# Masking the causal scores with pairs of half-array products of 256 columns

## The chip, the cores and the metric

The kernel runs on one core of one Trainium2 chip. The metric is the device time of one execution in microseconds (us). The engines are TensorE (PE, matmuls; PEld are its weight loads), VectorE (DVE), ScalarE (ACT), GpSimd (POOL) and SyncE (SP, which issues most DMAs). They run side by side and wait for each other on semaphores. TensorE's clock has two levels, 1.2 and 2.4 GHz; the profile gives the granted clock as a share of full speed.

## The reference

There are 32 sequences of 128 tokens with 128 features. Two layers follow each other, each a cross-attention to a context (16 heads of 8 features) and an expert network, and each adds to x. Only the second attention is causal:

```python
Q = (query @ Wq + bq).reshape(B, Tq, H, Hd).transpose(0, 2, 1, 3)
K = (key @ Wk + bk).reshape(B, Tk, H, Hd).transpose(0, 2, 1, 3)
scores = jnp.einsum('bhqd,bhkd->bhqk', Q, K) / scale
causal = jnp.triu(jnp.ones((Tq, Tk), bool), k=1)
scores = jnp.where(causal[None, None], -jnp.inf, scores)
attn = jax.nn.softmax(scores, axis=-1)
out = jnp.einsum('bhqk,bhkd->bhqd', attn, V)
...
x = x + _L0_xattn_ref(_layernorm(x), ctx_1024, ctx_1024, ...)
x = x + _L0_ffn_ref(_layernorm(x), ...)       # each token to one of 8 experts
x = x + _L1_xattn_ref(_layernorm(x), ctx_1024, ctx_1024, ...)   # causal
x = x + _L1_ffn_ref(_layernorm(x), ...)       # each token to two of 8 experts
```

## The kernel before, in words

The program has six parts, each a block that all engines enter and leave together: `prepare` (loads weights, makes constants), `project` (queries, keys and values), `attention(0)`, `experts0`, `attention(1)`, which is the causal one, and `experts1`. The order of the instructions is written out by hand in each engine's function. Semaphores alone hold the engines together.

`prepare` fills `ident4` (four identity matrices of 128x128 side by side, bf16) and `future` (row k, column q holds -1e30 where key k lies behind query q, else 0). SP issues 18 loads there and waits for them. PE then turns the weights over, DVE copies them out, and the block ends when the last engine is done.

In `attention(l)` the loop runs over n, the sequence. At step n, PE makes the scores of sequence n + 3 and the probabilities' products of sequences n and n - 1. A sequence is done in two units u = 0 and 1 of eight heads each. The steps of a unit are:

- `scores(n, u)` on PE. It waits for `max_s`, the maxima of the unit before, since all units share the two PSUM banks `s_pair`. In the causal layer a mask product comes first: for each of the two banks (four heads each), `future` as stationary operand by `ident4`, 128 rows and 512 columns (L628). Then come eight score products of 128 columns (L633), in pairs: `half(0, ...)` uses rows 0 to 63 of the array and writes bank 0, `half(1, ...)` uses rows 64 to 127 and writes bank 1. They add to the mask.
- `reduce_pair(n, u)` on DVE (L861) takes each row's maximum from the 1024 columns. It signals `max_s`.
- `scores_t(n, u)` on PE makes the same scores with keys on the rows (L654) and adds minus the maxima (L657), again in half-array pairs. It waits until the exponentials have freed its two banks.
- `exponential` on ACT (L763), `mask` on POOL (L1029, which sets the future to zero once more), and `mix` on PE (L670), the product with the values.

Between them stand the turning of the maxima (L642), of the outputs (L681, L688) and the output projection (L692). From the sixth sequence on, the routing of the second expert network is worked in, in batches of four sequences: L700, L706 on PE, a row of short DVE steps (L898 to L947), and scattered writes from POOL (L1058).

The names in the profile drop digits, so that `ident` in a row of L628 is `ident4`, and `rrrk` is `ranked`.

Of the kernel before, what the change touches and what calls it, by code (L numbers as in the profile page):

```python
# [136 lines left out]
def build(nc, a, out):  # L137
# [3 lines left out]
    def sem(name):  # L141
        in_use.append(nc.alloc_semaphore(name=name))
        return in_use[-1]
# [10 lines left out]
    with ctx:  # L154
        def sb(name, shape, dt=F32, to=ctx):
            return to.enter_context(nc.sbuf_tensor(name, shape, dt))
# [12 lines left out]
        ident = sb("ident", [128, 128])  # L169
        ident4 = sb("ident4", [128, 4, 128], BF16)  # L170
        future = sb("future", [128, 128], BF16)
        earlier_tokens = sb("earlier_tokens", [128, 128], BF16)
        all_tokens = sb("all_tokens", [128, 128], BF16)
        tile_no_i, tile_no = sb("tile_no_i", [128, SLOTS], I32), sb("tile_no", [128, SLOTS])
# [47 lines left out]
        def prepare():  # L222

            loaded, zeroed = sem("p_loaded"), sem("p_zeroed")
            turned, kept, made, counted = sem("p_turned"), sem("p_kept"), sem("p_made"), sem("p_counted")
            picked = sem("p_picked")
            with ExitStack() as own, nc.Block() as block:
                w_raw = [sb(f"w_raw{i}", [128, D], to=own) for i in range(4)]
                qk_raw = [sb(f"qk_raw{i}", [128, D], to=own) for i in range(2)]
# [14 lines left out]
                @block.sync  # L244
                def _(sp):
                    for to, src in loads:
                        sp.dma_start(to, src, allow_slow_non_contiguous=True).then_inc(loaded, 16)
                    sp.wait_ge(loaded, 16 * len(loads))

                @block.gpsimd  # L250
                def _(pool):
# [288 lines left out]
        def attention(l):  # L540
# [13 lines left out]
            with ExitStack() as own, nc.Block() as block:  # L554
# [41 lines left out]
                def half(a, rows):  # L596
                    return slice(a * HALF, a * HALF + rows)
# [5 lines left out]
                @block.sync  # L603
                def _(sp):
                    def load(g):
                        sp.wait_ge(st_ps, (g - QK_BUFS + 1) * G * PAIRS)
                        for side in "kq":
                            load_side(sp, l, g, side, qk_in[g % QK_BUFS])

                    for g in range(QK_BUFS, NG):  # L610
                        load(g)
                    for g in range(NG - QK_BUFS, NG):
                        sp.wait_ge(qk_in[g % QK_BUFS], g // QK_BUFS * QK_IN)

                @block.tensor
                def _(pe):
                    def scores(n, u):

                        buf, t = columns(n)
                        if u == 0 and n % G == 0:  # L620
                            if n // G < QK_BUFS:
                                pe.wait_ge(early_in[l], QK_BUFS * QK_IN)
                            else:
                                pe.wait_ge(qk_in[buf], n // G // QK_BUFS * QK_IN)
                        pe.wait_ge(max_s, earlier(n * PAIRS + u))
                        if causal:
                            for a in range(2):
                                pe.matmul(s_pair[:, a * 512:(a + 1) * 512], future[:],  # L628
                                          ident4[:].rearrange("p a b -> p (a b)"), start=True, stop=False,
                                          skip_group_check=True)  # L630
                        for j in range(C4):
                            for a in range(2):
                                mm = pe.matmul(s_pair[:, (a * C4 + j) * T:(a * C4 + j + 1) * T],  # L633
                                               qq[buf][half(a, PROD), u * C4 + j, t], kk[buf][half(a, PROD), u * C4 + j, t],
                                               start=not causal, stop=True, skip_group_check=causal)
                        mm.then_inc(s_ps, 1)
# [1027 lines left out]
```

## Time and profile before

| | |
|---|---|
| times of three runs | 892.91, 894.95, 895.14 us; median 894.95 |
| profiled execution | 895.08 us, of which the span is 893.3 |
| PE / PEld busy | 670.4 / 458.0 us |
| DVE / ACT / POOL busy | 483.9 / 385.5 / 347.6 us |
| L628, as many as are recorded | 98 matmuls of 128x512, 35.1 us, mean 417 ns |
| causal attention | 428 to 627 us of the span |

The profile is one execution. Busy time of PE is modelled from where a matmul starts and how long its columns take, so that starts are a better measure than durations: two matmuls that overlap both show their full latency. Some matmul records are missing. In the rows below, the bracket at the end names how long the engine was idle before the instruction and what ended that idle time; "issue" is idle time without a waited-for event. A row with "x2" or "x8" merges instructions, and its first number is the start of the first.

### The profile page before, as it was taken

What the parts mean: (1) busy time and instruction counts of PE and PEld (TensorE: products, weight loads), DVE (VectorE), ACT (ScalarE), POOL (GpSimd) and SP (SyncE); (2) the same over time, 40 slices, a digit from 0 to 9 for tenths busy, and PEclk for the clock granted to TensorE, in tenths of its full rate; (3) what the DMA queues carried; (4) which work ended last, traced back from release to release, by engine and by line L of the source; (5) the groups of instructions that cost most, each with busy time, mean ns of one, the idle gap of its engine ahead of it and who ended that gap; (6) DMA issues with size and microseconds to landing.
All of it is one profiled execution on the core that took longest, in us unless ns stands there. A gap on an engine that the chain in (4) does not pass through costs nothing. (4 is left out here: it accounts for less than half of the span.)

```text
span 893.3 us, 21719 instructions
## 1 busy us (share of the span) xinstructions
PE 670.4 (75%) x7687; PEld 458.0 (51%) x7717; DVE 483.9 (54%) x1275; ACT 385.5 (43%) x948; POOL 347.6 (39%) x506
## 2 busy tenths in 40 slices
PE   1566648898996898994499999998406999999910
PEld 1343326676774454541155666665304877787700
DVE  1687446676772677773356888887341222222213
ACT  0344325575774012121056666667303665666500
POOL 4354240010011134342034477778841544455410
PEclk9988677899998899997589999999556999999965
DMA  3459831464302999999014333300111222212027
GB/s 95 132 152 182 209 114 24 80 108 81 74 3 38 208 239 209 216 219 228 7 23 77 72 90 87 84 26 26 43 36 48 59 55 61 58 55 64 28 72 222
DMA packets 93273, 87.17 MB, mean 98 GB/s; under 512 B 7785, under 2 KB 87921, under 8 KB 90097
## 3 DMA queue, kind: packets, MB, share of 16 engines
q1 hardware_dynamic: 84592, 74.70, 38.9%
q0 software_dynamic: 4352, 8.99, 3.2%
q10 hardware_dynamic: 4224, 2.10, 0.8%
q8 instruction: 65, 1.06, 0.5%
q14 instruction: 40, 0.32, 0.1%
HBM read 43.99 MB, written 41.76 MB: 96 GB/s over the span
## 5 line engine op out<-in xcount | busy, mean ns | idle before, releaser
L861 DVE TENSOR_REDUCE nm<-bank 128x8 f32<-128x1024 f32 x128 | 156.5, 1223 | 63.8 <-PE bank L633 61.7
L763 ACT ACTIVATE pr<-bank 128x512 f32<-128x512 f32 x256 | 147.2, 604 | 85.0 <-PE bank L657 82.2
L1572 DVE TENSOR_TENSOR exac<-bank,exsi 128x352 f32<-128x352 f32 x72 | 37.8, 525 | 127.8 <-PE bank L1479 121.0
L1029 POOL TENSOR_SCALAR_AFFINE_SELECT pr<-pr 128x1024 f32<-128x1024 f32 x64 | 69.7, 1088 | 75.3 <-ACT pr L763 75.1
L1451 POOL DMA_INDIRECT results<-exy,exre x72 | 70.8, 983 | 33.0 <-issue 33.0
L670 PE MATMUL bank<-pr,values 128*9 128x128 f32 x2048 | 82.3, 280 | 1.7 <-POOL pr L1029 1.7
L654 PE MATMUL bank<-qq,kk 48*128 48x128 bf16 x1024 | 76.8, 223 | 6.4 <-issue 4.2
L1308 PE MATMUL bank<-e0ch,expert_w 128*128 128x512 f32 x128 | 71.9, 644 | 8.2 <-DVE e0ch L1220 8.1
L657 PE MATMUL bank<-mt,pick 64*128 64x128 bf16 x1024 | 76.8, 223 | 0.0
L633 PE MATMUL bank<-kk,qq 48*128 48x128 bf16 x1024 | 55.5, 233 | 19.5 <-DVE nm L861 8.0
L1058 POOL DMA_INDIRECT sorted_in<-rrrow,rrpli x64 | 63.2, 988 | 14.2 <-issue 14.0
L1493 PEld LDWEIGHTS bank<-down_w,exat 128*128 128x128 f32 (+1 forms) x432 | 58.9, 191 | 18.3 <-issue 6.7
L633 PEld LDWEIGHTS bank<-kk,qq 48*128 48x128 bf16 x1024 | 31.4, 100 | 66.9 <-issue 38.6
L1493 PE MATMUL bank<-down_w,exat 128*128 (+1 forms) x432 | 60.4, 276 | 1.9 <-ACT exat L1535 1.9
L1476 PE MATMUL bank<-gate_w,exxt 128*128 x144 | 57.9, 485 | 0.9 <-ACT exxt L1524 0.8
L628 PE MATMUL bank<-ident,future 128*128 128x512 bf16 x98 | 35.1, 417 | 28.2 <-DVE bank L985 11.1
L654 PEld LDWEIGHTS bank<-qq,kk 48*128 48x128 bf16 x1024 | 52.1, 98 | 7.9 <-issue 4.5
L1479 PE MATMUL bank<-up_w,exxt 128*128 x144 | 55.6, 469 | 0.0
L1036 POOL CAST mp<-nm 128x16 bf16<-128x16 f32 x32 | 6.3, 196 | 126.3 <-DVE nm L861 122.0
L657 PEld LDWEIGHTS bank<-mt,pick 64*128 64x128 bf16 x1024 | 52.3, 98 | 2.3 <-issue 2.3
L1544 ACT ACTIVATE exy<-bank,exsh 128x128 f32<-128x128 f32 x72 | 26.4, 367 | 61.5 <-PE bank L1493 52.4
L670 PEld LDWEIGHTS bank<-pr,values 128*9 128x9 f32 x2048 | 43.9, 91 | 15.6 <-POOL pr L1029 2.2
(203 smaller groups left out, 1304.3 us busy)
## 6 DMA issues: line engine op xcount, KB each, us to landing
sorted_in<-padding SPq DMA_DIRECT2D x8, 2145.0 KB
k_parts<-pj_parts SPq DMA_DIRECT2D x16, 384.0 KB, 2.9
kk<-k_parts SPq DMA_DIRECT2D x32, 192.0 KB
qq<-q_parts SPq DMA_DIRECT2D x32, 192.0 KB
exx<-sorted_in SPq DMA_DIRECT2D x72, 65.0 KB
kk<-k_parts SPq DMA_DIRECT2D x32, 128.0 KB
qq<-q_parts SPq DMA_DIRECT2D x32, 128.0 KB
coy<-results SPq DMA_DIRECT2D x8, 512.0 KB, 4.7
```

The source lines that it names most:

```text
L633: mm = pe.matmul(s_pair[:, (a * C4 + j) * T:(a * C4 + j + 1) * T], qq[buf][half(a, PROD), u * C4 + j, t], kk[buf][half(a, PROD), u * C4 + ...
L654: pe.matmul(to[a][:, j * T:(j + 1) * T], kk[buf][half(a, PROD), u * C4 + j, t], qq[buf][half(a, PROD), u * C4 + j, t], start=True, stop=Fa ...
L657: mm = pe.matmul(to[a][:, j * T:(j + 1) * T], pick[half(a, HALF), u * C4 + j, :], max_t[n % 3][half(a, HALF), :], start=False, stop=True, ...
L670: mm = pe.matmul(o_bank[32 * j:32 * j + VW, c * T:(c + 1) * T], values[l][:, n, c % 2 * H2 + c // 2 * C4 + j, :], probs[c][:, j * T:(j + 1 ...
L763: act.activation(probs[c], st_bank[(n * NC + c) % ST][:], ACT.Exp, scale=scale).then_inc(exp_s, 1)
L861: dve.tensor_reduce(neg_max[n % 2][:, u * 2 * C4:(u + 1) * 2 * C4], s_pair.rearrange("q (h k) -> q h k", k=T), AX_X, ALU.max, negate=True) ...
L1029: pool.affine_select(out=probs_pair[u][:], in_=probs_pair[u][:], compare_op=ALU.is_ge, fill=0.0, base=0, pattern=[[0, 2 * C4], [1, T]], ch ...
L1058: pool.indirect_dma_start(sorted_in[:], bass.IndirectOffsetOnAxis(ap=place_i[bt.p][:, k, b:b + 1], axis=0), row[bt.p][:, k, b, :], None).t ...
L1308: pe.matmul(y_bank[:], expert0_w[:, e, :], chosen[e % 2][:], start=(e == 0), stop=(e == E - 1)).then_inc(y_ps, 1)
L1451: pool.indirect_dma_start(results[:], bass.IndirectOffsetOnAxis(ap=result[q.g.p][:, q.b:q.b + 1], axis=0), y_g[q.p][:], None).then_inc(y_o ...
L1476: pe.matmul(gate_bank[q.p][:, 0:F], x, gate_w[:, bass.ds(e, 1), :].rearrange("d e f -> d (e f)"), start=True, stop=True).then_inc(gate_ps, 1)
L1493: mm = pe.matmul(y_bank[q.p][:, 0:D], acts_t[q.p][0:fn, f * T:(f + 1) * T], down_w[0:fn, bass.ds(e, 1), f, :].rearrange("f e d -> f (e d)" ...
```

## The change

The mask product of a unit is written as four matmuls of 64 rows and 256 columns. Each bank's mask is cut by keys: turn 0 covers keys 0 to 63 of each of the four heads, turn 1 covers keys 64 to 127. In each turn the half a = 0 of the array (rows 0 to 63) writes bank 0 and the half a = 1 (rows 64 to 127) writes bank 1. The stationary operand is `future_h`, which holds both 64-row halves of `future` on both halves of the partitions; the moving operand is `ident4h`, four identities of 64x64 on both halves. Both are filled in `prepare` by six small DMAs of SP, for which SP waits before it leaves the block.

```diff
@@ build
+        ident4h = sb("ident4h", [128, 4, HALF], BF16)
+        future_h = sb("future_h", [128, 2, 128], BF16)
@@ prepare, block.sync
                     sp.wait_ge(loaded, 16 * len(loads))
+                    sp.wait_ge(made, 4)
+                    for a in range(2):
+                        to = slice(a * HALF, (a + 1) * HALF)
+                        for k in range(2):
+                            of = slice(k * HALF, (k + 1) * HALF)
+                            sp.dma_start(future_h[to, k, :], future[of, :]).then_inc(halved, 16)
+                        sp.dma_start(ident4h[to, :, :], ident4[0:HALF, :, 0:HALF]).then_inc(halved, 16)
+                    sp.wait_ge(halved, 96)
@@ attention, block.tensor
+                    def hide(pair, of):
+                        for turn in range(2):
+                            for a in range(2):
+                                to = pair[a].rearrange("p (j c) -> p j c", c=T)
+                                pe.matmul(to[:, :, half(turn, HALF)], of[half(a, HALF), turn, :], ident4h[half(a, HALF), :, :],
+                                          start=turn == 0, stop=False, skip_group_check=True)
@@ scores
                         if causal:
-                            for a in range(2):
-                                pe.matmul(s_pair[:, a * 512:(a + 1) * 512], future[:],
-                                          ident4[:].rearrange("p a b -> p (a b)"), start=True, stop=False,
-                                          skip_group_check=True)
+                            hide([s_pair[:, a * 512:(a + 1) * 512] for a in range(2)], future_h)
```

On PE, one unit of the causal attention before, with the end of the unit ahead of it. L670 are the products with the values, L628 the mask, L633 the scores, L654 and L657 the transposed scores:

```order
L642 MATMUL bank<-ident,mp 128x128
L670 MATMUL bank<-pr,values 9x128 x8
L628 MATMUL bank<-ident,future 128x512 x2
L633 MATMUL bank<-kk,qq 128x128 x8
L654 MATMUL bank<-qq,kk 128x128 x2
L657 MATMUL bank<-mt,pick 128x128 x2
```

The same place after. The lines have moved by the inserted ones: L657, L685, L632, L648, L669 and L672 answer to the six above.

```order
L657 MATMUL bank<-ident,mp 128x128
L685 MATMUL bank<-pr,values 9x128 x8
L632 MATMUL bank<-ident4h,future_h 128x4x64 x4
L648 MATMUL bank<-kk,qq 128x128 x8
L669 MATMUL bank<-qq,kk 128x128 x2
L672 MATMUL bank<-mt,pick 128x128 x2
```

The mask stands where it stood, and four narrower products take the place of two.

On SP, the end of `prepare` before, with the last load, and the first load of `project`:

```order
L247 DMA bo1<-L1_xattn_bo 128x128
L227 UNCONDITIONAL_BRANCH [waits p_loaded]
L378 UNCONDITIONAL_BRANCH [waits barrier_Pool_Activation_PE_DVE_SP_release]
L382 DMA pj_c0<-ctx_1024 128x4x128 [waits pj_c_turned]
```

And after:

```order
L249 DMA bo1<-L1_xattn_bo 128x128
L256 DMA future_h<-future 64x128 [waits p_made,p_loaded]
L256 DMA future_h<-future 64x128
L257 DMA ident4h<-ident4 64x4x64
L256 DMA future_h<-future 64x128 x2
L257 DMA ident4h<-ident4 64x4x64
L229 UNCONDITIONAL_BRANCH [waits p_halved]
L388 UNCONDITIONAL_BRANCH [waits barrier_Pool_Activation_PE_DVE_SP_release]
L392 DMA pj_c0<-ctx_1024 128x4x128 [waits pj_c_turned]
```

Six DMAs and one wait have come between the last load and the end of the block.

## Rows read from the trace of the kernel before

Times in the timelines are the start and the duration in us from the span's start. The rows by stretch give the stretch and its length, then busy us (and instructions) of PE, PEld, DVE, ACT and POOL, the granted clock, the share of the DMA engines and GB/s.

**Rows 1.** Busy time by stretch of the causal attention.
```profile
428.00:453.00 25.00, 15.65 (x145) 6.70 (x149) 10.43 (x15) 3.11 (x9) 1.91 (x2) 0.52 0.00 1
...
457.00:497.00 40.00, 37.87 (x695) 24.34 (x703) 26.86 (x63) 25.06 (x66) 17.50 (x18) 1.00 0.41 77
...
497.00:609.00 112.00, 101.44 (x1833) 68.17 (x1846) 99.08 (x281) 70.49 (x183) 80.82 (x86) 1.00 0.29 65
...
609.00:627.00 18.00, 13.98 (x257) 10.12 (x255) 11.67 (x48) 12.92 (x31) 14.91 (x16) 1.00 0.09 29
```

**Rows 2.** Timeline of the opening: start us, us, engine, line, op, tiles.
```profile
431.16 1.04 PE L628 MATMUL bank<-ident,future 128*128 128x512 bf16 x2 [1.39 <-DVE nm L861]
...
432.13 0.61 PE L633 MATMUL bank<-kk,qq 48*128 48x128 bf16 x8
...
432.78 1.22 DVE L861 TENSOR_REDUCE nm<-bank 128x8 f32<-128x1024 f32 x1 [1.68 <-PE bank L633]
...
434.06 1.04 PE L628 MATMUL bank<-ident,future 128*128 128x512 bf16 x2 [1.33 <-DVE nm L861]
```

**Rows 3.** Timeline of one sequence of the second stretch.
```profile
473.50 1.23 DVE L861 TENSOR_REDUCE nm<-bank 128x8 f32<-128x1024 f32 x1 [1.14 <-PE bank L633]
...
474.70 0.61 ACT L763 ACTIVATE pr<-bank 128x512 f32<-128x512 f32 x1
...
474.78 0.61 PE L628 MATMUL bank<-ident,future 128*128 128x512 bf16 x2
...
475.31 0.23 PEld L633 LDWEIGHTS bank<-kk,qq 48*128 48x128 bf16 x8 [0.42 <-issue]
...
475.50 0.10 PEld L654 LDWEIGHTS bank<-qq,kk 48*128 48x128 bf16 x2
...
475.55 0.22 PE L654 MATMUL bank<-qq,kk 48*128 48x128 bf16 x2
...
475.61 0.22 PE L657 MATMUL bank<-mt,pick 64*128 64x128 bf16 x2
...
475.76 1.22 DVE L861 TENSOR_REDUCE nm<-bank 128x8 f32<-128x1024 f32 x1 [0.41 <-PE bank L633]
...
478.75 1.22 DVE L861 TENSOR_REDUCE nm<-bank 128x8 f32<-128x1024 f32 x1 [1.14 <-PE bank L633]
```

**Rows 4.** Waits from 490 to 600 us: total us, times, longest.
```profile
DVE nm L861 <- PE bank L633: 9.3, 12, 1.1
```

**Rows 5.** Timeline of the third stretch, start of a batch.
```profile
560.74 0.61 PE L628 MATMUL bank<-ident,future 128*128 128x512 bf16 x2 [0.27 <-DVE nm L861]
...
562.35 1.21 DVE L861 TENSOR_REDUCE nm<-bank 128x8 f32<-128x1024 f32 x1
...
563.72 0.11 PEld L628 LDWEIGHTS bank<-ident,future 128*128 128x128 bf16 x2 [0.22 <-issue]
...
564.70 1.23 DVE L861 TENSOR_REDUCE nm<-bank 128x8 f32<-128x1024 f32 x1 [0.66 <-PE bank L633]
...
566.56 0.62 ACT L763 ACTIVATE pr<-bank 128x512 f32<-128x512 f32 x1
...
567.24 0.10 PEld L654 LDWEIGHTS bank<-qq,kk 48*128 48x128 bf16 x2
...
569.41 0.19 DVE L912 TENSOR_REDUCE rrhigh<-bank 128x4 f32<-128x32 f32 x1 [0.53 <-PE bank L706]
```

**Rows 6.** Timeline of the third stretch, POOL beside DVE.
```profile
546.02 1.09 POOL L1029 TENSOR_SCALAR_AFFINE_SELECT pr<-pr 128x1024 f32<-128x1024 f32 x1
...
546.37 0.80 DVE L914 TENSOR_TENSOR rrrk<-rrrk,expert_rank 128x32 f32<-128x32 f32 x1
```

**Rows 7.** Timeline of the program's start.
```profile
9.79 0.43 SPq L247 DMA_DIRECT2D bo<-L_xattn_bo  x1
...
12.80 0.71 PEld L293 LDWEIGHTS bank<-ident,w_raw 128*128 128x128 f32 x4 [12.80 <-DMA bo<-L_xattn_bo]
...
17.86 0.15 DVE L314 COPY gate_w<-bank 128x8 f32<-128x8 f32 x1
```

More of the change, by code:

```diff
@@ L225, in prepare @@
             turned, kept, made, counted = sem("p_turned"), sem("p_kept"), sem("p_made"), sem("p_counted")
-            picked = sem("p_picked")
+            picked, halved = sem("p_picked"), sem("p_halved")
             with ExitStack() as own, nc.Block() as block:
```

## The prediction

> **What bounds the kernel now.** I read the page first. Its slices put the changed line, L628, in one stage only: the causal attention, from 428 to 627 us of the span. The chain of work that ended last covers only the combination of the experts' outputs at the very end, so it says nothing here. I therefore cut the stage into stretches and read each by busy time [rows 1].
>
> In the opening TensorE (PE) is busy 15.65 of 25 us at a mean granted clock of 0.52. From 457 to 497 it is busy 37.87 of 40 us at full clock. From 497 to 609, where the routing work joins, it is busy 101.44 of 112 us and VectorE (DVE) 99.08. Two engines near full means that neither share alone decides; the waits inside a sequence do.
>
> There is one pair of banks for the row maxima. So mask product, scores, max reduction and the next mask product form a ring, and each sequence goes round it twice (64 rounds, which I call units). In the opening the ring is all there is: mask at 431.16, scores at 432.13, reduction at 432.78 to 434.00, next mask at 434.06 [rows 2]. A unit is 2.90 us, and the mask product owns 432.13 - 431.16 = 0.97 of it.
>
> Between 457 and 497 the reductions alternate at 2.26 and 2.99 us (473.50, 475.76, 478.75), DVE idles 0.41 and 1.14 us ahead of them for L633, and PE works almost without a gap [rows 3]. The first distance is the ring: the mask at 474.78 waited for the reduction. The second is PE's own list of work. Here the mask product owns 475.31 - 474.78 = 0.53 us.
>
> From 497 on, DVE waits for L633 only 12 times in 110 us, 9.3 us together [rows 4]. Those fall where a group's four sequences begin (564.70, 0.66 us) [rows 5]. Elsewhere DVE goes from one instruction to the next, and a shorter mask product meets nobody who waits.
>
> **The change part by part.** It removes 2 matmuls of 512 columns a unit and adds 4 of 256, in two pairs; the halves of a pair use different rows of the array and different banks. Four weight loads stand where two stood. Waits and order are the same.
>
> What a pair costs: the scores are such pairs already. An L654 pair begins at 475.55 and the L657 pair behind it at 475.61, so two half-array products of 128 columns take 0.06 us together [rows 3]. Two of 256 then take 0.11 to 0.12. The loads of 475.50 show 0.05 us ahead of the first matmul, and later ones hide behind the running pair. A unit's mask is 0.05 + 2 x 0.115 = 0.28 us, where it was 0.53: 0.25 us saved at full clock. At half clock the columns take twice as long: 0.05 + 2 x 0.21 to 0.22 = 0.48 against 0.97, 0.49 us saved. Bounds of the unit: if halves do not overlap, 4 x 0.107 (256 columns at 2.4 GHz) + 0.05 = 0.48 and almost nothing is saved; if the load hides fully, 0.23, and 0.30 is saved.
>
> Part of the 0.53 is no streaming: two 512-column products would need 4 times the 0.107 of 256 columns, 0.43, so 0.10 is the load and the passage from whole to half array [rows 3]. The Trainium skill (TensorEngine Tiling (Array Packing), Key Properties) says that a change of tiling mode drains TensorE. By that rule the passage behind the mask goes, since mask and scores now share a mode; it is included in my 0.25, and counting columns alone would give 0.21.
>
> Opening: 8 masks from 428 to 450 lie on the ring, 8 x 0.49 = 3.9 us. A mean clock of 0.52 over 25 us, with levels 0.5 and 1.0, leaves 1 us at full clock, so it rises at about 452 [rows 1]; the ninth mask lies across that and gives 0.3. Sum 4.2.
>
> Second stretch, 8 sequences. The mask in PE's own list gives 0.25. The mask on the ring gives less, because ScalarE (ACT) is next: the transposed scores behind it begin at 475.50, and the exponential that frees their banks ends at 474.70 + 0.61 = 475.31, with some 0.06 us for the signal 475.37 [rows 3]. Only 0.13 of the 0.25 passes. So 8 x 0.38 = 3.0, and 0.25 for the last unit before the routing: 3.3 us. Bounds: 2.0 (only the first kind) and 4.2 (both in full).
>
> Third stretch, 4 batches of four sequences that begin with a DVE wait. The mask at 560.74 was released by DVE and gains 0.25 in itself. The next could be loaded at 563.72 - 0.25, but the reduction ends at 562.35 + 1.21 = 563.56, so it starts at 563.61, 0.11 early, and saves its own 0.25. The reduction of 564.70 comes 0.36 early, inside its idle 0.66. At the third mask ACT closes the path: its exponential ends at 566.56 + 0.62 = 567.18 and PE goes on at 567.24 [rows 5]. So the routing scores that DVE awaits at 569.41 come 0.36 early, not 0.6. 4 x 0.36 = 1.4 us; bounds 0 and 2.6 (4 x 0.64).
>
> In the rest of a batch something else may move. DVE's L914, 0.80 us long, ends at 547.17, as GpSimd's (POOL) select does (546.02 + 1.09 = 547.11) [rows 6]: it was held. I count five such held operations in a batch, some 3.2 us together. Three of the selects waited for ACT, which now gets its banks 0.2 to 0.26 us earlier against DVE, so up to 0.7 us a batch comes back over 4.8 batches (3.4 us), or nothing, or new operations are hit. I take 1.5. The Trainium skill (SBUF — State Buffer, Who interferes with whom) tells the same lock: a DVE operation with two SBUF inputs and a GpSimd one that reads SBUF exclude each other. The trace agrees in these two ends.
>
> Start of the program: SP now issues six small DMAs once the loads have landed, at 12.8 us, at 0.43 us each as its last load [rows 7]: 12.8 + 2.6 = 15.4. Landing as long after issue as that load (9.79 to 12.80, 3.0 us, from the last issue at 15.0) gives 18.0. DVE holds the block open until 17.86 + 0.15 = 18.01 anyway. With a slower landing it costs something: I take 0.2 us, bounds 0 and 1.5.
>
> Sum: 4.2 + 3.3 + 1.4 + 1.5 - 0.2 = 10.2 us. The profiled execution took 895.08 (span 893.3 and 1.8 around it), 0.13 above the median of the three runs, 894.95. Forecast: 895.08 - 10.2 = 884.9. Behind the stage nothing changes: POOL's moves of rows and the experts begin that much earlier.
>
> **The rivals.**
> A: only the chains without DVE gain. The third stretch gives 0 and the ports 0; 4.2 + 3.3 - 0.2 = 7.3, or 887.8 (895.08 - 7.3). For it: DVE at 99.08 of 112 us.
> B: halves gain no time. Each writes four runs of 64 columns with gaps, which no matmul in this trace does. If the gaps cost as much as the overlap brings, the unit stays at 0.48: 64 x 0.05 = 3.2, a third of it off the path, minus 0.2: 893. The Trainium skill (PSUM — Partial Sum Buffer, Specifications (TRN2)) says that non-contiguous access slows matmuls significantly. Against it: every run is 64 adjacent values.
> C: ports fully relieved and the ACT gate moved with the rest: 4.2 + 4.2 + 1.4 + 3.4 - 0.2 = 13.0, or 882.1.
> D, slower: the selects fall onto DVE's short operations. There are 8 a batch, each 1.09 us; if each held DVE for 0.9 it would be 7.2 us for today's 3.2, 4.0 more. Over 4.8 batches that is 19 us lost against 4.2 + 3.3 + 1.4 - 0.2 = 8.7 gained: 905.4. It decides from 1.8 us a batch. Against it: DVE's order and its waits pin most of the pattern.
> The clock is in the range, not a case. PE held full clock at 13.98 busy of 18 us late in the stage [rows 1], a lower share than I expect anywhere after the opening. But the rise at 452 may come some us earlier or later against the work, and a unit at half clock costs about 0.7 us more: 1.5 us either way.
>
> **How the numbers follow.** Forecast 0.58, A 0.18, C 0.08, B 0.10, D 0.06. A difference under 0.3% (2.7 us) is what a measurement of this kernel cannot tell from none. Forecast, A and C are faster, together 0.84; nearly all of B and an edge of A are same, 0.10; D is slower, 0.06. The range leaves out B and D and reaches below C, since the clock moves each: 880.5 to 890.5.
>
> **What the profile after would show.** Mask to first score product 0.28 us at full clock and 0.48 at half; units of 2.4 us in the opening for 2.90; sequences of 4.9 us for 5.25 in the second stretch; four sequences in the third stretch 0.3 to 1.0 us shorter; L861's idle for L633 smaller; the first block's end at most 0.3 us later. The mechanism is wrong if the mask takes 0.45 us or more, and the sizes are wrong if the third stretch alone moves by over 5 us or the opening stays at 2.9.

## The result and the profile after

Times in us; the ratio is that of this kernel to the kernel before on the same chip, with its 95% interval.

| | before | after |
|---|---|---|
| median | 894.5 (16 runs) | 888.6 (16 runs) |
| profiled execution, its span | 895.08, 893.3 | 891.50, 889.8 |
| ratio | | 0.9934 (0.9909 to 0.9960) |

The medians are those of all runs; the ratios here and below leave out runs over 1.5% above the fastest of their kernel (2 of 16 here, 5 of 12 in after_again, its profiled one among them, 2 of 12 in tag_first, 1 of 6 in warm_again and in moves_late).

The gain is 5.9 us, 0.66%. The forecast was 10.2 us and 884.9; the median lies inside the range (880.5 to 890.5) and nearest to rival A (887.8). All lines below `hide` stand 15 further down: L633 is now L648, L654 is L669, L657 is L672, L861 is L876; the mask product is L632.

First two of the stretches of [rows 1]. Columns: stretch, its length, busy time of PE, PEld, DVE, ACT and POOL, granted clock, DMA share, GB/s.

```profile
457.00:497.00 40.00, 38.42 (x786) 28.29 (x783) 29.96 (x74) 27.50 (x72) 18.78 (x19) 1.00 0.43 82
497.00:609.00 112.00, 94.11 (x1850) 70.55 (x1846) 93.83 (x270) 69.49 (x179) 79.80 (x84) 0.97 0.30 64
```

From 457 to 497 DVE is busy 29.96 us for 26.86, as more units pass. From 497 to 609 it is busy less (93.83 for 99.08), and the mean granted clock is 0.97 for 1.00. A stretch that was at full clock no longer is: that is where to look.

The opening, as [rows 2]:

```profile
431.63 0.61 PE L632 MATMUL bank<-ident4h,future_h 64*128 64x256 bf16 x4 [1.39 <-DVE nm L876]
...
432.04 0.63 PE L648 MATMUL bank<-kk,qq 48*128 48x128 bf16 x8
...
432.71 1.23 DVE L876 TENSOR_REDUCE nm<-bank 128x8 f32<-128x1024 f32 x1 [1.14 <-PE bank L648]
...
434.00 0.61 PE L632 MATMUL bank<-ident4h,future_h 64*128 64x256 bf16 x4 [1.33 <-DVE nm L876]
```

Mask to first score takes 0.41 us for 0.97, and a unit 2.36 for 2.90. One sequence of the second stretch, as [rows 3]:

```profile
469.78 1.23 DVE L876 TENSOR_REDUCE nm<-bank 128x8 f32<-128x1024 f32 x1 [0.82 <-PE bank L648]
...
471.06 0.39 PE L632 MATMUL bank<-ident4h,future_h 64*128 64x256 bf16 x4
...
471.29 0.39 PE L648 MATMUL bank<-kk,qq 48*128 48x128 bf16 x8
...
471.72 1.22 DVE L876 TENSOR_REDUCE nm<-bank 128x8 f32<-128x1024 f32 x1
...
474.54 1.22 DVE L876 TENSOR_REDUCE nm<-bank 128x8 f32<-128x1024 f32 x1 [0.82 <-PE bank L648]
```

The mask takes 0.23 us for 0.53. The reductions are 1.94 and 2.82 us apart for 2.26 and 2.99; the one at 471.72 has no idle time any more, so the ring has become as short as DVE allows. Then the third stretch, at the 43rd unit (reductions at 538.20 and 545.99, 7.79 us; the same unit took 3.70 before):

```profile
538.34 0.22 PE L669 MATMUL bank<-qq,kk 48*128 48x128 bf16 x1
...
540.97 0.21 PE L669 MATMUL bank<-qq,kk 48*128 48x128 bf16 x1 [2.41 <-issue]
```

TensorE stops in the middle of a group of sixteen matmuls that wait for nothing, for 2.41 us. "issue" says that no event of the profile ended it. Behind it the granted clock is at the lower level for 6 us (0.51). The unit is 4.0 us longer than the 3.78 of the same place in later batches, and its whole batch takes 27.74 us for 23.37 to 23.41, so a stop costs 4.3 us here:

```profile
536.00:540.00 4.00, 2.42 (x48) 1.57 (x43) 2.80 (x8) 2.58 (x7) 3.23 (x4) 1.00 0.62 120
542.00:548.00 6.00, 6.00 (x74) 4.29 (x74) 2.74 (x9) 2.57 (x7) 2.25 (x3) 0.51 0.05 15
```

One more wait has grown, at the start of a batch. ACT's exponential behind its laying of rows (L804, before L789) comes late. Before:

```profile
545.81 0.63 ACT L789 COPY rrrow<-rrrow 128x512 f32<-128x512 f32 x1
...
548.13 0.60 ACT L763 ACTIVATE pr<-bank 128x512 f32<-128x512 f32 x1 [1.69 <-PE bank L657]
```

After:

```profile
567.90 0.63 ACT L804 COPY rrrow<-rrrow 128x512 f32<-128x512 f32 x1
...
568.11 1.09 POOL L1044 TENSOR_SCALAR_AFFINE_SELECT pr<-pr 128x1024 f32<-128x1024 f32 x1
...
569.37 0.97 POOL L1073 DMA_INDIRECT sorted_in<-rrrow,rrpli  x1 [0.17 <-issue]
...
570.76 0.60 ACT L778 ACTIVATE pr<-bank 128x512 f32<-128x512 f32 x1 [2.23 <-PE bank L672]
...
571.48 0.17 DVE L898 TENSOR_TENSOR mp<-nm,mp 128x16 bf16<-128x16 f32 x1 [0.54 <-ACT mp L815]
```

2.23 us behind the laying's end for 1.69, and the matmuls it waits for ended at 569.86 already. DVE waits 0.54 us for ACT. All waits of [rows 4] now:

```profile
DVE nm L876 <- PE bank L648: 6.8, 12, 1.3
```

The start of the program, as [rows 7]: the six loads go out from 12.80 to 16.64 (rows marked x2 hold two of them), 0.62 us each for the 0.43 of the sum. They land 1.8 to 1.9 us after issue (median) for the 3.0 assumed. DVE's last copy ends at 18.05 for 18.01.

```profile
12.80 1.19 SPq L256 DMA_DIRECT2D future_h<-future  x2
...
16.02 0.62 SPq L257 DMA_DIRECT2D ident4h<-ident  x1
...
17.89 0.16 DVE L324 COPY gate_w<-bank 128x8 f32<-128x8 f32 x1
```

The 64 reductions are the ruler for all that follows. Each number is a distance between starts in one profiled execution: R0 is the first reduction, and the unit R42 is the distance from R41 to R42, the 43rd reduction. R0 to R10 is the opening, R10 to R25 the second stretch, R25 to R63 the third. A batch is eight reductions of the third; R33 to R41, R41 to R49 and R49 to R57 are shown. "Late" says whether the exponential behind the laying comes 2.2 us or more after the laying's end in the batches behind the first.

| kernel | R0-R10 | R10-R25 | R25-R63 | batches | late | units of over 5 us |
|---|---|---|---|---|---|---|
| before | 27.88 | 39.41 | 112.07 | 23.40, 23.40, 23.49 | no | none |
| after | 25.15 | 35.99 | 116.43 | 23.41, 27.74, 23.37 | yes | R42 7.79 |
| before_again | 27.92 | 39.40 | 113.61 | 23.80, 23.79, 23.78 | yes | none |
| after_again | 24.71 | 36.34 | 120.04 | 23.41, 29.59, 25.01 | yes | R42 7.21, R49 5.35, R50 5.53 |
| unit1_only | 26.52 | 37.91 | 111.74 | 23.40, 23.47, 23.40 | yes | none |
| whole_array | 27.57 | 39.49 | 118.18 | 23.82, 28.25, 23.82 | yes | R42 7.88 |
| tag_first | 24.98 | 35.99 | 120.78 | 23.38, 30.59, 24.86 | yes | R42 8.59, R49 5.27, R50 5.36 |
| pad64 | 25.61 | 39.22 | 112.17 | 23.39, 23.43, 23.38 | yes | R18 5.81 |
| warm | 22.30 | 37.15 | 112.60 | 23.42, 23.62, 23.35 | yes | none |
| warm_again | 22.04 | 37.69 | 112.99 | 23.38, 23.47, 23.39 | yes | none |
| warm_before | 24.82 | 39.40 | 115.79 | 23.79, 24.50, 25.22 | yes | none |
| moves_late | 25.16 | 36.00 | 125.72 | 28.37, 25.91, 26.97 | not all | none |

### The profile page after: what moved, and what is told of

Its sections match the earlier page's. It is cut to its first block and busy times, and to the rows that moved or that the text cites. A ratio compares the mean times of both kernels' runs of the same rounds, so it can differ in the third digit from the quotient of the medians.

```text
span 889.8 us, 22012 instructions
## 1 busy us (share of the span) xinstructions
PE 659.4 (74%) x7845; PEld 466.9 (52%) x7845; DVE 482.4 (54%) x1275; ACT 387.3 (44%) x948; POOL 347.7 (39%) x506
## 5 line engine op out<-in xcount | busy, mean ns | idle before, releaser
L876 DVE TENSOR_REDUCE nm<-bank 128x8 f32<-128x1024 f32 x128 | 156.5, 1223 | 55.3 <-PE bank L648 53.1
L669 PE MATMUL bank<-qq,kk 48*128 48x128 bf16 x1024 | 77.8, 225 | 12.8 <-issue 7.2
L685 PE MATMUL bank<-pr,values 128*9 128x128 f32 x2048 | 83.5, 283 | 1.9 <-POOL pr L1044 1.5
L672 PE MATMUL bank<-mt,pick 64*128 64x128 bf16 x1024 | 77.7, 224 | 0.0
L648 PE MATMUL bank<-kk,qq 48*128 48x128 bf16 x1024 | 56.0, 234 | 19.4 <-DVE bank L1000 8.0
L669 PEld LDWEIGHTS bank<-qq,kk 48*128 48x128 bf16 x1024 | 52.1, 99 | 14.9 <-ACT pr L778 7.0
L648 PEld LDWEIGHTS bank<-kk,qq 48*128 48x128 bf16 x1024 | 38.3, 102 | 38.8 <-DVE nm L876 20.4
L672 PEld LDWEIGHTS bank<-mt,pick 64*128 64x128 bf16 x1024 | 52.6, 99 | 4.8 <-issue 4.8
L685 PEld LDWEIGHTS bank<-pr,values 128*9 128x9 f32 x2048 | 44.3, 91 | 16.5 <-issue 3.0
L1235 DVE TENSOR_TENSOR e0ch<-bank,e0xt 128x512 f32<-128x512 f32 x64 | 42.6, 678 | 6.2 <-PE bank L1314 6.2
```

What stands on the lines that cost most here:

```text
L669: pe.matmul(to[a][:, j * T:(j + 1) * T], kk[buf][half(a, PROD), u * C4 + j, t], qq[buf][half(a, PROD), u * C4 + j, t], start=True, stop=Fa ...
L672: mm = pe.matmul(to[a][:, j * T:(j + 1) * T], pick[half(a, HALF), u * C4 + j, :], max_t[n % 3][half(a, HALF), :], start=False, stop=True, ...
L685: mm = pe.matmul(o_bank[32 * j:32 * j + VW, c * T:(c + 1) * T], values[l][:, n, c % 2 * H2 + c // 2 * C4 + j, :], probs[c][:, j * T:(j + 1 ...
L876: dve.tensor_reduce(neg_max[n % 2][:, u * 2 * C4:(u + 1) * 2 * C4], s_pair.rearrange("q (h k) -> q h k", k=T), AX_X, ALU.max, negate=True) ...
```

## The experiments

**before_again, after_again: the two kernels once more, unchanged.**

> The kernel before once more, for a second trace. Theory 1 (the third stretch keeps nothing because of DVE's and ACT's order of work): the distances of the reductions are those of the first trace, 2.90 in the opening, 2.26 and 2.99, then 23.4 us a batch. Theory 2 (the third stretch's loss is an accident of one execution): batches vary here too by over 0.5 us.

> The changed kernel once more, for a second trace and 5 rounds. In its first trace the third stretch gained nothing and PE stood for 2.4 us without a waited-for event near 541, with the clock at half for some us behind it. Theory 1: batches are again 23.3 to 23.5 us, and the exponential behind the laying of rows again comes 0.9 us late; without the pause the stage is 4 us shorter than in the first trace. Theory 2: batches are 22.9 us or less. Ratio 0.990 to 0.995 by either.

Measured: before_again 900.43 us in one run. after_again 890.01 us (12 runs), ratio 0.9910 (0.9872 to 0.9949). With all runs in, the medians 890.01 and 894.5 (29 runs of the kernel before on that chip) are 0.995 apart, so 0.9910 is the more favourable of two readings. The regular distances of opening and second stretch repeat to 0.01 us (2.90; 2.26 and 2.99; 2.36; 1.94 and 2.82); in after_again R9 and R10 were shorter (2.74 and 2.16 for 3.01 and 2.33) and one unit of the second stretch longer (3.67). Two things do not belong where I had put them. The late exponential is in the kernel before too, in this execution:

```profile
551.70 0.63 ACT L789 COPY rrrow<-rrrow 128x512 f32<-128x512 f32 x1
...
553.17 0.97 POOL L1058 DMA_INDIRECT sorted_in<-rrrow,rrpli  x1 [0.17 <-issue]
...
554.59 0.60 ACT L763 ACTIVATE pr<-bank 128x512 f32<-128x512 f32 x1 [2.26 <-PE bank L657]
```

Its batches are 23.79 us then, and those of the kernel after 23.41 with the same lateness. So the change gives 0.38 us a batch, like for like, and my first trace of the kernel before was the one without the lateness. Two more kernels with whole-array masks, below, have late batches of 23.8 us as well (whole_array 23.82, warm_before 23.79), and those with pairs 23.4. And the stop of TensorE comes again at R42 in the kernel after, with a second one at 564.46:

```profile
537.87 0.21 PE L669 MATMUL bank<-qq,kk 48*128 48x128 bf16 x1 [1.65 <-issue]
...
564.46 0.40 PE L685 MATMUL bank<-pr,values 128*9 128x128 f32 x7 [2.52 <-issue]
```

**unit1_only: pairs for every second unit, the old product for the others.**

```diff
-                            hide([s_pair[:, a * 512:(a + 1) * 512] for a in range(2)], future_h)
+                            if u == 1:
+                                hide([s_pair[:, a * 512:(a + 1) * 512] for a in range(2)], future_h)
+                            else:
+                                for a in range(2):
+                                    pe.matmul(s_pair[:, a * 512:(a + 1) * 512], future[:],
...
```

> Half-array pairs in the unit u = 1 alone, the old product in u = 0. In the second stretch u = 1's mask waits for the reduction (the ring), u = 0's comes out of PE's own list. Theory 1: the ring's distance falls from 2.26 to 1.94, the other one, which ACT's exponential ends, from 2.99 to 3.15 or more, so a sequence gets 0.13 to 0.2 us shorter; the opening gains 0.27 us a unit on average (half of 0.54). Rival: the two edits are independent, a sequence gains 0.31 (half of the 0.6 that PE gets back).

Measured: 889.88 us (12 runs), ratio 0.9957 (0.9927 to 0.9987). The opening alternates 2.36 and 2.90. In the second stretch the ring's distance is 1.94 and the other 3.14: 5.08 a sequence for 5.25. The ring's unit comes 0.32 earlier, but 0.15 of it is lost again at the next: alone it is worth 0.17. The trace shows where:

```profile
475.27 0.61 ACT L784 ACTIVATE pr<-bank 128x512 f32<-128x512 f32 x1
...
475.94 0.23 PE L675 MATMUL bank<-qq,kk 48*128 48x128 bf16 x2
```

The transposed scores (L675) begin 0.06 us after the exponential ended (475.88). They stand 0.36 us behind the scores of 475.58, where in the kernel before they follow after 0.23 (475.32, 475.55): 0.13 is lost at ACT. The 0.32 to the 0.49 of the full change is what the list's unit is worth. No stop in the stage. From R0 to R63 this trace is shorter (176.17 us) than both of the kernel after (177.57 and 181.09), and the medians of the two kernels on this chip are the same, 889.88 and 890.01: half of the pairs brought as much as all of them with the stop.

**whole_array: the same four products of 256 columns, on the whole array.**

```diff
-                                pe.matmul(to[:, :, half(turn, HALF)], of[half(a, HALF), turn, :], ident4h[half(a, HALF), :, :],
+                                pe.matmul(to[:, :, half(turn, HALF)], future[:], ident4[:, :, half(turn, HALF)],
```

> Four products of 256 columns a unit as in the changed kernel, with the same gaps in the output, but each on the whole array (all 128 rows of future, strided identity), so that no two overlap. Theory 1 (the overlap of the halves is the gain): mask to first score 0.5 to 0.55 us at full clock and 0.95 at half, the time that of before within 1 us. Rival (fewer or narrower products, or their place in the array's mode, bring it without overlap): mask to score 0.3 to 0.45 and several us faster than before. If gaps in the output cost something, it is over 0.6.

Measured: 894.13 us (10 runs), ratio 0.9995 (0.9965 to 1.0026). Count, shape and the gaps between runs of 64 columns are those of the change, the overlap is not there, and with it the gain is gone:

```profile
470.23 0.61 PE L632 MATMUL bank<-ident,future 128*128 128x256 bf16 x4
...
470.77 0.40 PE L648 MATMUL bank<-kk,qq 48*128 48x128 bf16 x8
...
471.21 1.23 DVE L876 TENSOR_REDUCE nm<-bank 128x8 f32<-128x1024 f32 x1 [0.41 <-PE bank L648]
...
547.20 0.21 PE L669 MATMUL bank<-qq,kk 48*128 48x128 bf16 x1 [1.79 <-issue]
```

0.54 us from mask to score, as with two products of 512: four loads and writes with gaps cost nothing. The last row shows something else. This kernel has as many matmuls as the kernel after and stops at the same unit R42, without any pairs. Its median is still that of the kernel before (894.13 and 894.5). If the stop fell in every execution it should be some 4 us more, so it probably does not.

**tag_first: GpSimd's numbering of rows ahead of its selects.**

```diff
+                        for bt in BATCHES if causal else ():
+                            if n == bt.turns(0):
+                                tag(bt)
                         if causal and seq(n):
                             mask(n, 0)
```

> The changed kernel with POOL's iota of the row tags moved from behind the second select of its step to ahead of the first. In the changed kernel's traces, and in the second trace of the kernel before, ACT's first exponential behind the laying of rows starts 0.9 us after its scores are ready, and each time 0.20 to 0.23 us after that iota's end. Theory 1 (POOL's iota holds ACT there): the exponential follows the scores at once, a batch falls from 23.4 to 22.8 us, the stage is 2 to 2.5 us shorter. Rival (the iota only happens to end there; the delay has another cause, such as the indirect DMA ahead of it): the exponential is as late as before and the batch stays at 23.4.

Measured: 891.67 us (12 runs), ratio 0.9951 (0.9913 to 0.9989). The exponential still comes 2.27 us after the laying (509.05 to 511.32) with the numbering long done. The numbering does not hold it.

**pad64: 64 matmuls of 8 columns more in `prepare`.**

```diff
+                    for _ in range(64):
+                        pe.matmul(bank[4][:, 0:8], ident4[:, 0, :], ident4[:, 0, 0:8], start=True, stop=True)
```

> The changed kernel with 64 tiny products (8 columns) more on PE in the first block, behind the last transpose, where PE waits for DVE. The three traces with four mask products a unit all have a pause of PE without a waited-for event of 1.7 to 2.4 us at the 43rd reduction of the stage (that unit 7.2 to 7.9 us instead of 3.8); the three with fewer instructions have none there. Theory: PE runs out of instructions, and the fetch of the next ones meets the loads of queries and keys; 128 more instructions ahead move the fetches, the pause vanishes or moves to another unit, and without one the stage is 4.3 us shorter. Rival: the pause belongs to the place in the stage (the loads themselves); it stays at the 43rd unit.

Measured: 887.24 us (12 runs), ratio 0.9941 (0.9913 to 0.9969). R42 takes 3.76 us. The stop has moved to R18, in the second stretch, and takes the clock down there:

```profile
474.55 0.33 PE L705 MATMUL bank<-ident,on 128*128 128x128 f32 x1 [1.78 <-issue]
```

```profile
474.00:480.00 6.00, 5.39 (x80) 3.82 (x80) 2.03 (x5) 2.53 (x8) 1.09 (x1) 0.72 0.14 31
```

From 455 to 473 it had been 1.00. With 64 matmuls more at the start of the program the stop is gone from R42 and one stands at R18, so the place goes by how many instructions PE has run. The next experiment bears that out. But the stage has a say in whether the stop comes: moves_late, the last experiment, has the very instructions of the kernel after on PE, and R42 passes there in 3.11 us without a stop. The interval overlaps with that of the kernel after: moving the stop is no gain that these runs can tell.

**warm: TensorE kept busy ahead of the stage and in its opening.**

```diff
+                        if causal and 0 < n * PAIRS + u < 9:
+                            for _ in range(4):
+                                pe.matmul(r_bank[:], ident4[:, 0, :], ident4[:].rearrange("p a b -> p (a b)"),
+                                          start=True, stop=True)
                         pe.wait_ge(max_s, earlier(n * PAIRS + u))
...
                     queries(LAST)
+                    for _ in range(26):
+                        pe.matmul(hot_bank[0][:], ident4[:, 0, :], ident4[:].rearrange("p a b -> p (a b)"),
+                                  start=True, stop=True)
```

> The changed kernel with idle TensorE time filled: 26 products of 512 columns behind PE's last work in the block before the stage, and 4 ahead of each of units 1 to 8, whose results nobody reads. It asks whether the opening's 2.36 us a unit are the half clock's. Theory: the clock is at full when the stage begins or within a few units; the opening's units fall to 1.94, the units behind them are at full clock at once, the stage is 4 to 5 us shorter. Rival 1: the clock does not hold; the 4 products at half clock take 1.7 us where the reduction gives 1.3, units of 2.8 us, and the stage is 2 to 4 us longer. Rival 2: the pause near the 43rd unit moves, since PE has 116 instructions more; then up to 4 us shorter for that alone.

Measured: 883.83 us (6 runs), ratio 0.9896 (0.9867 to 0.9924). The opening's units take 1.94 us once the clock is full, and R0 to R10 is 22.30 for 25.15. The second rival came true beside it: R42 takes 3.95 us without a stop, and one has come to R18 (3.96 us; 4.51 in warm_again, where it lasts 1.43):

```profile
462.68 0.38 PE L711 MATMUL bank<-wo,ont 128*128 128x128 f32 x1 [0.88 <-issue]
```

By then this kernel has run 58 matmuls more than the kernel after, and pad64 64 more. Its stop stands six matmuls further on than that of pad64 (behind one of L707, four of L700 and one of L711), which is just that difference. So warm is not a price of warming alone. From R0 to R63 its trace is 5.5 us shorter than that of the kernel after: 2.9 in the opening and 3.8 in the third stretch, where the stop is missing, less 1.2 in the second. Against pad64, on the same chip and without the stop at R42 too, the median is 3.4 us lower, and the intervals of the two ratios just overlap.

**warm_before, warm_again: the same warming on the kernel before, and warm once more beside it.**

> The kernel before (mask product on the whole array, 2 x 512 columns) with the same warming as `warm`: 26 products behind the last queries, and four ahead of the maxima's wait in units 1 to 8 of the causal stage. Theory: the pairs' gain is 0.31 us a unit wherever TensorE has full clock and the unit is a ring (mask to first score 0.54 for 0.23), 0.54 a unit at half clock. The opening, being warmed, then gives only 8 x 0.31 = 2.5 us instead of 4.3, the second stretch its 3.4, the third about nothing. Expected: opening units of 2.26 us once the clock is full (warm: 1.94); 883.8 + 5.9 = 889.7 us, a ratio to the kernel before of 0.994. Rival: warming replaces the pairs' gain (what the pairs gave was mostly half-clock time): then this kernel is within 2 us of warm, 884 to 886. Rival 2: the warming only helps with pairs (its own products are in the way on a whole-array list): 894, no gain.

> The same kernel as warm, on the same chip as warm_before: 883.8 us again, 878 to 887. Units of the opening at 1.94 us once the clock is full. If the 10 us gain of the first run was chance of a chip, it comes out at 888 or more.

Measured on one chip: warm_before 890.69 us (12 runs), ratio 0.9976 (0.9946 to 1.0007); warm_again 882.04 us (6 runs), ratio 0.9886 (0.9843 to 0.9929). warm_before, then warm_again:

```profile
434.49 1.23 DVE L865 TENSOR_REDUCE nm<-bank 128x8 f32<-128x1024 f32 x1 [0.95 <-PE bank L637]
...
435.77 0.61 PE L632 MATMUL bank<-ident,future 128*128 128x512 bf16 x2 [0.35 <-DVE nm L865]
436.31 0.40 PE L637 MATMUL bank<-kk,qq 48*128 48x128 bf16 x8
...
436.75 1.23 DVE L865 TENSOR_REDUCE nm<-bank 128x8 f32<-128x1024 f32 x1 [1.04 <-PE bank L637]
```

```profile
428.99 0.39 PE L632 MATMUL bank<-ident4h,future_h 64*128 64x256 bf16 x4 [0.35 <-DVE nm L880]
429.21 0.39 PE L652 MATMUL bank<-kk,qq 48*128 48x128 bf16 x8
...
429.64 1.23 DVE L880 TENSOR_REDUCE nm<-bank 128x8 f32<-128x1024 f32 x1 [0.64 <-PE bank L652]
```

Both at full clock: 2.26 a unit against 1.94, 0.54 from mask to score against 0.22. In the opening the pairs give 24.82 - 22.04 = 2.78 us. The two medians are 8.6 us apart, the two traces 7.3 between R0 and R63 (the forecast was 5.9); 2.0 of that are two units (R42, R50) of 4.79 and 4.73 us in warm_before that pass in 3.79 and 3.75 in warm_again, so I do not put all of it down to the pairs. The first rival (warming replaces the pairs' gain) is out, since the medians on one chip are 8.6 us apart where it had under 2; that warming by itself gives more than 1 us is not shown.

**moves_late: GpSimd's first scattered write of a sequence behind its second select.**

```diff
-                        moves(n, 0)
                         if causal and seq(n):
                             mask(n, 1)
+                        moves(n, 0)
                         moves(n, 1)
```

> The kernel after, in which GpSimd runs the select of the unit u = 1 ahead of the first scattered write of a sequence instead of behind it (the two writes of a sequence then stand together behind both selects). What it is for: in every late case the exponential behind ACT's laying of rows (L804) starts 0.41 to 0.45 us after GpSimd's indirect DMA has ended, 2.26 us after the laying instead of 1.69. Theory DMA: the write holds ACT (or what ACT waits for). The write now starts only after the select of u = 1, which waits for the very exponential, so no write lies in front of it: exponential 1.5 to 1.7 us after the laying's end, and 0.57 us a batch of four sequences come back (batches of 22.8 for 23.4), if nothing else takes the place; 886 to 888 us. Rival: the lateness has another cause (code, or a fixed time of ACT): still 2.26 after the laying, batches of 23.4, 888 to 890. Price either way: the moves end up to 2 us later behind the last sequence.

Measured: 901.72 us (6 runs), ratio 1.0107 (1.0058 to 1.0157), 10 us slower than the kernel before. Neither theory had that. Two scattered writes now stand in a row ahead of the next sequence's select. The exponential that this select awaits ended at 540.91, but the second write runs until 541.88:

```profile
539.58 1.04 POOL L1073 DMA_INDIRECT sorted_in<-rrrow,rrpli  x1 [0.17 <-issue]
...
540.29 0.62 ACT L778 ACTIVATE pr<-bank 128x512 f32<-128x512 f32 x1
...
540.92 0.96 POOL L1073 DMA_INDIRECT sorted_in<-rrrow,rrpli  x1 [0.30 <-issue]
...
541.89 1.11 POOL L1044 TENSOR_SCALAR_AFFINE_SELECT pr<-pr 128x1024 f32<-128x1024 f32 x1
```

So a select, and the product with the values behind it, starts 1 us after it could, and batches take 25.9 us and more. It did not part the theories either: the writes of the sequence before now stood in the gap, and the exponential was late again (2.17 and 2.94 us).

## Why the prediction was right and wrong

**The mask of a unit: right, and a little better.** 0.28 was forecast at full clock and 0.23 measured; 0.48 at half clock and 0.41 measured. The load that I had added ahead of the first pair does not show; two pairs of 256 columns are 2 x 0.107 and 0.02 more. The 0.10 us that I had read as load and passage from whole to half array is gone with it: 0.54 - 0.23 = 0.31, of which columns alone explain 0.21. Rival B, gaps that cost what the overlap brings, falls by whole_array, which has the gaps and takes no longer than two products of 512. The Trainium skill (PSUM — Partial Sum Buffer, Specifications (TRN2)) says that non-contiguous access slows matmuls significantly; runs of 64 values with gaps of 64 did not, 0.54 us with them and 0.54 without.

**The opening: 4.2 forecast, 3.3 measured** (2.73 from R0 to R10 and 0.54 in the first unit). The term per unit was right (0.54 for 0.49), eight of them gave 4.3. What failed is the ninth term, "the ninth mask lies across that and gives 0.3". I had tied the clock's rise to a place of the work. It came at nearly the same time as before: in the microsecond from 452 in the first trace of the kernel before, and in that from 453 in the first of the kernel after, which is 22 to 23 us behind R0 in both, and in their second traces (granted clock 0.50 in the microsecond before, 0.88 and 0.81 in these, 1.00 behind them). There the mask of 452.28 was the first at full clock. Now the work was 3 to 4 us further on:

```profile
452.10 0.61 PE L632 MATMUL bank<-ident4h,future_h 64*128 64x256 bf16 x4
...
454.84 0.39 PE L632 MATMUL bank<-ident4h,future_h 64*128 64x256 bf16 x4
```

The mask of 452.10 is still at half clock. The three units behind R7 took 3.29, 3.01 and 2.33 us for 2.85, 2.26 and 2.47, and 1.05 us of the gain was given back.

**The second stretch: 3.3 forecast, 3.4 measured.** Seven sequences lie between R10 and R25, at 0.49 each for the 0.38 forecast. The gate at ACT that I had read is real (0.13 lost there in unit1_only): the ring's mask is worth 0.17, where I had 0.13, and so the list's 0.32, where I had 0.25. Both are larger because the mask itself gave 0.31.

**The third stretch and the ports: 1.4 and 1.5 forecast, 1.5 measured for both together,** and most of that is the ports' term. The total is that of late traces compared with late ones: 113.61 us from R25 to R63 in before_again, and 116.43 less the 4.3 of the stop in the kernel after. Against the first trace of the kernel before, the batches are the same length (23.40). There the late exponential (0.4 us a batch) was absent, and it was present in every other kernel of the table but moves_late, where it was mixed.

What fails is the step "the routing scores that DVE awaits at 569.41 come 0.36 early", for the starts of batches. The reduction of that place does come early: 2.01 us behind the one ahead of it for 2.32. But the next two distances are 2.76 for 2.64 and 3.78 for 3.70, and with them 0.20 of the 0.31 is given back.

The ports' term came out nearly as forecast, at one of the five held operations. Before (before_again), then after:

```profile
587.87 1.09 POOL L1029 TENSOR_SCALAR_AFFINE_SELECT pr<-pr 128x1024 f32<-128x1024 f32 x1 [0.65 <-ACT pr L763]
587.92 1.07 DVE L945 TENSOR_SCALAR rrdiff<-rrden 128x4 f32<-128x4 f32 x1
```

```profile
579.94 1.08 POOL L1044 TENSOR_SCALAR_AFFINE_SELECT pr<-pr 128x1024 f32<-128x1024 f32 x1 [0.33 <-ACT pr L778]
580.23 0.82 DVE L958 CAST rrpli<-rrplace 128x8 int32<-128x8 f32 x1
```

The select waits for ACT 0.33 us for 0.65. It now starts 0.29 ahead of the DVE operation that it holds, and both end together again: that operation is held for 0.82 us in place of 1.07 (in the first trace of the kernel before it was L943, with 1.10). L945 or L943 takes 0.16 to 0.17 when nothing holds it. DVE is busy without a gap from reduction to reduction there, and that distance is 3.08 us in both traces of the kernel after, where it is 3.34 to 3.37 in both of the kernel before and 3.33 to 3.37 in whole_array. It occurs five times from R25 to R63: 5 x 0.26 = 1.3 us. The operation of [rows 6] is held as before, until the select of 568.11 ends at 569.20:

```profile
568.46 0.80 DVE L929 TENSOR_TENSOR rrrk<-rrrk,expert_rank 128x32 f32<-128x32 f32 x1
```

**What no step had: the stop of TensorE.** In each of the two traces of the kernel after, R42 takes 7.79 and 7.21 us for 3.70. It costs 4.3 us in the first (the batch of 27.74 us), which is more than the third stretch and the ports gained. The change itself brought it there, since it doubles the number of mask products, 128 more matmuls: whole_array has the same count and the same stop, both traces of the kernel before and unit1_only have none in the stage, and pad64 and warm, with still more matmuls, have it elsewhere. It is not bound to come: moves_late, with the same list on PE, passes R42 without it, and the second stop of after_again (R49 and R50) is absent in the first trace. With 3.3 + 3.4 + 1.5 - 4.3 the stage gives 3.9 like for like, and 8.2 without the stop; between the medians lie 5.9, with an interval of 3.6 to 8.1. How often the stop falls in runs that were not profiled is open, and so is what it is. That PE waits for its own instructions fits all that was seen (the engine idles amid a group, on no event, at a place that goes by the count, and in some timings not at all; the kernel before has such stops too, 2.10 us at 165.85 and 2.13 us at 205.57 in its first attention), but no record of such a fetch was read.

**The start: 0.2 forecast, 0.04 measured**, in the end of DVE's last copy; the first load of `project` goes out 0.06 later (18.36 for 18.30).

The forecast was thus right in sign and in the mechanism of the mask, and 4.3 us too high. 0.9 of that is the clock's edge and 1.4 the starts of batches with the ports (2.9 forecast, 1.5 measured). The second stretch and the start were 0.3 better than forecast, so the terms that were measured sum to 8.2. The rest, 2.3, is less than a stop costs. It fits a stop in part of the executions. It would fit as well that the kernel before runs without the late exponential in part of its own, as it did in one of its two traces, which takes up to 1.6 us from the gain. Both are argued and not shown. That rival A's number fits is chance: its reason (the third stretch and the ports give nothing) is what a comparison of two single traces would say, and the second trace of the kernel before contradicts it.

Left open: what holds ACT's exponential. In the late cases in which its matmuls had long ended, it starts 0.38 to 0.49 us after the end of the scattered write in the gap, with one exception (1.15). In the others (behind a stop, and in two batches of warm_before) its matmuls ended late themselves. But the write alone does not hold it: in the first trace of the kernel before it stood at the same place (laying's end 569.94, write 570.78 to 571.75), and the exponential started at 571.62, before the write had ended. A kernel without that write would tell more; it was not tried.

## What to carry to other kernels

A short product that fills the array's rows can be cut by its contraction into two half-array streams on two banks whenever its neighbours run in halves already. It pays by the overlap, here 0.31 us of 0.54 at full clock. Count it only where the engine's list or a ring through it sets the pace, and recount at the edge where the granted clock changes: a saving ahead of the clock's rise is partly paid back behind it. A term under a few us is to be read against two traces of the kernel before, because one trace can differ from the next by a fixed wait in each batch. The lowest medians are those of the pairs with a warmed TensorE, 882.0 and 883.8 us. They are clearly below the kernel before. No run of the kernel after on their chips is on record, the intervals of the ratios overlap with those of the kernel after, and part of their gain is the stop that moved. Count the matmuls that a change adds as well: here they brought a stop into a stage that had none, and 64 matmuls of padding moved it.

## What was not expected of the hardware

- TensorE stops within groups that wait for nothing: in the causal stage for 1.65 to 2.75 us at R42, R49 and R18, and shorter in moves_late (1.22), warm and warm_again (0.88, 1.43). The place goes with the number of its instructions: R42 with two mask products more in each unit than the kernel before, R18 with 64 or 58 more still, ahead of the stage or in its opening, and these two six matmuls apart. Whether it comes also hangs on the timing, since moves_late has none at R42. After the stop of 2.41 us the granted clock stood at 0.51 for 6 us, and the whole cost 4.3.
- Two half-array streams of 256 columns on two banks take about the time of one: two pairs take 0.23 us, where 2 x 0.107 is what two streams of 256 columns need at 2.4 GHz. The same work on the whole array took 0.54. The outputs had runs of 64 columns in both.
- Idle TensorE between short groups keeps half clock for 25 us of the opening; products that do nothing but fill the gaps bring the full clock to it (0.93 as the mean of the 26 us, for 0.50), and the opening becomes 2.9 us shorter:

```profile
427.00:453.00 26.00, 15.45 (x205) 10.34 (x207) 12.18 (x17) 4.94 (x14) 3.10 (x5) 0.50 0.01 2
```

```profile
420.00:446.00 26.00, 21.12 (x309) 12.04 (x316) 14.12 (x19) 6.36 (x17) 4.73 (x6) 0.93 0.01 2
```
